# A two-layer transformer kernel: the first expert layer over tokens sorted by expert, with indirect DMAs

## The reference, cut to what matters

```python
n = layernorm(x)
x = x + attention_0(n) + experts_0(n)   # 8 heads, latent keys and values of 32, softmax over 1024
n = layernorm(x)
x = x + flow_attention_1(n) + experts_1(n)   # sums over tokens, no softmax; 8 experts, top 4, limits and biases

# experts_0: 8 experts, F = 256; each token t goes to two experts e with weights g from the router
y[t] = sum_e g[t, e] * (silu(n[t] @ w_gate[e].T) * (n[t] @ w_up[e].T)) @ w_down[e].T
```

## Time and profile before

| | |
|---|---|
| median of 3 runs | 3385.93 us (3384.25 to 3387.49) |
| the profiled execution | 3380.49 us |
| its span, first to last instruction | 3378.7 us |
| TensorE busy | 3081.9 us, 91% |
| VectorE busy | 2275.8 us, 67% |
| ScalarE busy | 1506.6 us, 45% |
| GpSimd (POOL) busy | 757.3 us, 22% |
| mean granted TensorE clock | 0.962 of 2.4 GHz |
| moved by DMA | 165.66 MB, 49 GB/s |

### The profile page before, as it was taken

One profiled execution on the slowest core, in us unless ns is written; L12 is line 12 of the kernel. 1 busy time (PEld: TensorE's weight loads), 2 busy tenths in 40 slices (PEclk: granted clock), 3 DMA queues, 4 the chain that ended last, 5 costly groups with the idle time before them and its releaser, 6 DMA issues.

```text
span 3378.7 us, 66006 instructions
## 1 busy us (share of the span) xinstructions
PE 3081.9 (91%) x21792; PEld 2160.6 (64%) x21792; DVE 2275.8 (67%) x3629; ACT 1506.6 (45%) x2490; POOL 757.3 (22%) x566
## 2 busy tenths in 40 slices
PE   4999789997899988999889988899889998999988
PEld 2776557765577655776567755677566775667755
DVE  3774677747776477764877648775497755977558
ACT  2663246722366224662246523565225642266422
POOL 0005230052300432004410134101350023500325
PEclk8999899998999999999999989999899998999989
DMA  5002110022100221002210012001120011200112
GB/s 213 8 27 76 60 48 8 27 75 70 44 3 30 72 82 33 27 10 67 85 30 27 21 56 91 24 27 32 45 94 21 27 45 63 69 15 27 57 57 69
DMA packets 81782, 165.66 MB, mean 49 GB/s; under 512 B 8271, under 2 KB 26904, under 8 KB 80920
## 3 DMA queue, kind: packets, MB, share of 16 engines
q1 hardware_dynamic: 81432, 161.11, 14.6%
HBM read 147.97 MB, written 13.11 MB: 48 GB/s over the span
## 4 chain that ended last, share of the span: by engine, by line
PE 72%; DVE 12%; issue 9%; ACT 3%; POOL 1%; DMA 1%; DVEq 1%; POOLq 0%; ACTq 0%; SPq 0%
PE ps L1146 17%; PE ps L1208 15%; PE ps L1227 12%; PE ps L1153 9%; PE ps L1241 8%; PE ps L1260 3%; DVE ffn_u L959 1%; PE ps L1173 1%; DVE probsT L977 1%; PE ps L1117 1%; DVE ffn_gu L1061 1%; DVE neg_max L857 1%; PE ps L1319 1%; ACT q_parts L565 1%; POOL probs L492 1%
## 5 line engine op out<-in xcount | busy, mean ns | idle before, releaser
L492 POOL TENSOR_TENSOR probs<-ffn_gu,gate_bc 128x512 f32<-128x512 f32 x416 | 555.1, 1336 | 2351.6 <-DVE ffn_gu L920 1843.0
L1146 PE MATMUL ps<-x_parts,w_split 128*128 128x512 f32 x3072 | 946.7, 444 | 82.8 <-DVE ffn_u L959 59.5
L1146 PEld LDWEIGHTS ps<-x_parts,w_split 128*128 128x128 f32 x3072 | 566.8, 189 | 399.9 <-issue 223.1
L857 DVE TENSOR_REDUCE neg_max<-ps 128x1 f32<-128x1024 f32 x512 | 626.0, 1223 | 237.0 <-PE ps L1208 141.1
L595 ACT ACTIVATE probs<-ps,neg_max 128x1024 f32<-128x1024 f32 x512 | 572.1, 1117 | 240.9 <-DVE neg_max L857 240.9
L1208 PE MATMUL ps<-keys,q_parts 128*128 128x512 f32 x2048 | 612.5, 421 | 21.1 <-DVE q_parts L850 11.4
L1227 PE MATMUL ps<-ident,probs 128*128 128x128 f32 x4096 | 543.1, 274 | 15.0 <-DVE probsT L868 13.9
L1227 PEld LDWEIGHTS ps<-ident,probs 128*128 128x128 f32 x4096 | 476.8, 141 | 104.2 <-DVE probsT L868 26.3
L1153 PE MATMUL ps<-probs,w_down 128*128 128x512 f32 x832 | 431.1, 604 | 46.0 <-POOL probs L492 45.2
L1208 PEld LDWEIGHTS ps<-keys,q_parts 128*128 128x128 f32 x2048 | 345.1, 188 | 168.9 <-issue 99.0
L920 DVE TENSOR_TENSOR ffn_gu<-ffn_s,ps 128x512 f32<-128x512 f32 x256 | 175.8, 687 | 330.7 <-ACT ffn_s L620 163.8
(11 more groups left out here) (171 smaller groups left out, 2517.5 us busy)
## 6 DMA issues: line engine op xcount, KB each, us to landing
w_split<-w_parts SPq DMA_DIRECT2D x260, 256.0 KB, 2.6
gate_bc<-gate_rows SPq DMA_DIRECT2D x128, 512.0 KB, 4.1
w_parts<-q_parts SPq DMA_DIRECT2D x4, 2048.0 KB, 9.3
x_in<-in_x SPq DMA_DIRECT2D x9, 512.0 KB, 3.7
out<-x_mid SPq DMA_DIRECT2D x8, 512.0 KB, 3.4
probsT<-in_gate_up SPq DMA_DIRECT2D x1, 2048.0 KB, 8.2
gate_bc<-in_gate_up SPq DMA_DIRECT2D x1, 2048.0 KB, 12.5
w_down<-in_down SPq DMA_DIRECT2D x2, 1024.0 KB
```

Of the source, the lines that this page charges most:

```text
L492: nc.gpsimd.tensor_tensor(ffn_h[u % 5], ffn_gu[:, u % 3, :], gate_bc[:, e % GATE_SLOTS, c * BANK:(c + 1) * BANK], ALU.mult).then_inc(h_rea ...
L857: nc.vector.tensor_reduce(neg_max[:, t % 4:t % 4 + 1], banks(2 * (t % 2)), X, ALU.max, negate=True).then_inc(max_ready.sem, 1)
L1146: mm = nc.tensor.matmul(ps[:, bank, :], w_split[:, f % 4, h, k * P:(k + 1) * P], tokens[:, half], start=(part == 0), stop=(part == 2))
```

## The change

- **Sorting.** The router now also marks the two experts chosen by each token. TensorE counts, with the matrices `before` and `ones`, how many earlier tokens chose the same expert. From that VectorE works out (`places`, two operations per step from step 40 on) a row number for each of the 2048 pairs of token and expert, such that every expert's rows begin at a multiple of 128, and for each of 23 blocks of 128 rows the number of its expert.
- **Scatter.** POOL writes the normed tokens to `x_rows` in HBM with 16 indirect DMAs of 128 rows. SP loads all 2944 rows back as `xs`.
- **Blocks** (`chosen_experts`). For each of 23 blocks TensorE reads the number of its expert from SBUF into a register (`value_load`) and makes three products with the tokens as the stationary and the weights as the moving operand, 512 columns (both halves of gate and up). The weights of layer 0 stay in SBUF (`w_res`). Silu and product are over 128x256, then two transposes, a copy, and two down products over 128 columns. Each group of four blocks has its tokens transposed and split ahead.
- **Back.** Each group's outputs are copied and stored to `y_rows`. When all six stores have landed, POOL reads them with 16 indirect DMAs, and VectorE multiplies by the token's two weights and adds.
- **Gone from layer 0**: the gates' transposes, their rows in HBM and the multiplication on POOL, the chunks of weights, and the transposes of the sums.
- **Attention.** `values` has two pieces of 32 matmuls in steps two apart. Where an instruction waits for two semaphores, the wait that is met earlier now stands first. VectorE's router operation stands behind the copy instead of ahead of it.
- **Memory.** `gate_bc`, `x_high` and `x_low` share memory with `q_parts`, and `xT` of layer 1 with `probsT`. The preparation splits the weights of layer 1 only by way of `w_prep`.

```diff
+BLOCKS = (2 * SEQ + E * (P - 1)) // P
+BLOCK_GROUPS = -(-BLOCKS // 4)
+TRANSPOSE_LAG = 2
+BLOCK_DOWN_LAG = 4
+GATHERS = 4
...
 SP, in the loop
+                sp.wait_ge(scattered.sem, scattered.at(b, 16 * 2 * NT))
+                sp.sem_inc(rows_complete.sem, 1)
+                sp.dma_start(xs, x_rows[:, :].rearrange("(j p) d -> p j d", p=P)).then_inc(xs_loaded.sem, 16)
+                for q in range(BLOCK_GROUPS):
+                    part = group_blocks(q)
+                    sp.wait_ge(ys_ready.sem, ys_ready.at(b, q + 1))
+                    sp.dma_start(y_rows[part[0] * P:(part[-1] + 1) * P, :].rearrange("(j p) d -> p j d", p=P),
+                                 ys[:, part[0]:part[-1] + 1, :]).then_inc(ys_stored.sem, 16)
...
 POOL, in the loop
+                pool.wait_ge(pos_ready.sem, pos_ready.at(b, 1))
+                nc.gpsimd.tensor_tensor(pool_spare[:, 0:1], minus_half[:, 0:1], minus_half[:, 0:1], ALU.mult)
+                for k in range(2):
+                    for n in range(NT):
+                        nc.gpsimd.indirect_dma_start(
+                            out=x_rows[:, :], out_offset=bass.IndirectOffsetOnAxis(pos_i[:, k * NT + n:k * NT + n + 1], 0),
+                            in_=x_norm[0][:, n, :], in_offset=None).then_inc(scattered.sem, 16)
+                inverse_deviation(b, 1)
+                pool.wait_ge(ys_stored.sem, ys_stored.at(b, 16 * BLOCK_GROUPS))
+                nc.gpsimd.tensor_tensor(pool_spare[:, 1:2], minus_half[:, 0:1], minus_half[:, 0:1], ALU.mult)
+                for n in range(NT):
+                    for k in range(2):
+                        nc.gpsimd.indirect_dma_start(
+                            out=y_pair[:, k, n, :], out_offset=None, in_=y_rows[:, :],
+                            in_offset=bass.IndirectOffsetOnAxis(pos_i[:, k * NT + n:k * NT + n + 1], 0)
+                        ).then_inc(gathered[n * GATHERS // NT].sem, 16)
+                inverse_deviation(b, 2)
...
 VectorE, behind the blocks
-                experts_add(0)
+                for i in range(GATHERS):
+                    tiles = range(i * NT // GATHERS, (i + 1) * NT // GATHERS)
+                    dve.wait_ge(gathered[i].sem, gathered[i].at(b, 16 * 2 * NT // GATHERS))
+                    for n in tiles:
+                        last = nc.vector.scalar_tensor_tensor(x_mid[:, n, :], y_pair[:, 0, n, :], r_s1[:, n:n + 1],
+                                                              x_mid[:, n, :], ALU.mult, ALU.add)
+                    link(last)
...
 TensorE, chosen_experts
+                def gate_up(j):
+                    if j % 4 == 0:
+                        pe.wait_ge(xs_low_ready.sem, xs_low_ready.at(b, j // 4 + 1))
+                    if j >= 2:
+                        pe.wait_ge(block_done.sem, block_done.at(b, j - 1))
+                    at = slice(j * P, (j + 1) * P)
+                    for part, (h, x) in enumerate(((0, 0), (0, 1), (1, 0))):
+                        mm = nc.tensor.matmul(ps[:, j % 2, :], xs_parts[x][:, at],
+                                              w_res_flat[:, bass.ds(first[j] * 4 + h * 2 * F, 2 * F)],
+                                              start=(part == 0), stop=(part == 2))
+                    mm.then_inc(block_mm.sem, 1)
...
+                for j in range(BLOCKS + BLOCK_DOWN_LAG):
+                    if j < BLOCKS:
+                        first[j] = pe.value_load(block_i[0:1, j:j + 1], min_val=0, max_val=(E - 1) * FH * D)
+                        gate_up(j)
+                    if j % 4 == 1 and j // 4 + 1 < BLOCK_GROUPS:
+                        tokens(j // 4 + 1)
+                    if 0 <= j - TRANSPOSE_LAG < BLOCKS:
+                        turn(j - TRANSPOSE_LAG)
+                    if j >= BLOCK_DOWN_LAG:
+                        down(j - BLOCK_DOWN_LAG)
+                    beside(j)
...
 TensorE, attention
-                    for k in (2 * i, 2 * i + 1):
+                    for k in range(4 * i, 4 * i + 4):
...
-                    for i in range(4):
-                        g = group_at(w, VALUES_LAG + i)
+                    for i in range(2):
+                        g = group_at(w, VALUES_LAG + 2 * i)
...
 VectorE, attention_step, one of the reordered pairs
-                        dve.wait_ge(scores_ready.sem, scores_ready.at(b, t + 1))
                         if t >= 4:
                             dve.wait_ge(exp_done.sem, exp_done.at(b, t - 3))
+                        dve.wait_ge(scores_ready.sem, scores_ready.at(b, t + 1))
```

More of the change, by code:

```diff
@@ L151, in two_layer_kernel @@
         x_mid = sb("x_mid", [P, NT, D])
-        xT = [sb(f"xT{l}", [P, SEQ]) for l in range(2)]
+        xT_first = sb("xT_first", [P, SEQ])
         stats = sb("stats", [P, NT, 6])
@@ new lines, in two_layer_kernel @@
+        gate_bc = q_flat[:, 0:GATE_SLOTS * SEQ].bitcast(F32).rearrange("p (s c) -> p s c", s=GATE_SLOTS)
+        gate_rows = nc.dram_tensor("gate_rows", (E, SEQ), F32, kind="Internal").ap()
+        ffn = sb("ffn", [P, 12, BANK])
+        ffn_flat = ffn[:, :, :].rearrange("p a b -> p (a b)")
+        w_raw = [v.rearrange("p (f c) -> p f c", c=2 * P) for v in (room[:, 4 * SEQ:8 * SEQ], ffn_flat[:, 0:4 * SEQ])]
+        ffn_s, ffn_g, ffn_gu = ffn[:, 0:3, :], ffn[:, 3:6, :], ffn[:, 6:9, :]
+        ffn_u = [ffn[:, 9, :], ffn[:, 10, :], out_room[:, :, :, :].rearrange("p a b c -> p (a b c)")]
@@ L234, in two_layer_kernel @@
+        xs_parts = [q_flat[:, h * 4 * SEQ:h * 4 * SEQ + ROWS] for h in range(2)]
+        ys = probs[:, :, :].rearrange("p a b -> p (a b)")[:, 0:ROWS].rearrange("p (j d) -> p j d", d=D)
+        y_pair = room[:, 5 * SEQ:7 * SEQ].rearrange("p (k n d) -> p k n d", k=2, d=D)
         ident = sb("ident", [P, P])
@@ L386, in _ @@
                          ).then_inc(x_loaded.sem, 16)
-            for l in range(2):
+            for l in (1, 0):
                 sp.dma_start(w_raw[l], ins[f"gate_up{l}"].rearrange("p f a b -> p f (a b)")).then_inc(raw_in[l].sem, 16)
@@ L442, in _ @@
+                for e in range(GATE_SLOTS):
+                    load_row(e)
+                for f in range(CHUNK_SLOTS, CHUNKS + CHUNK_SLOTS):
+                    if f % FH == 0 and GATE_SLOTS <= f // FH < E:
+                        load_row(f // FH)
+                    sp.wait_ge(gu_ready.sem, gu_ready.at(b, (f - CHUNK_SLOTS + 1) * HALVES))
+                    load_chunk(f)
                 sp.wait_ge(y_added.sem, y_added.at(b, 4))
@@ new lines, in outputs @@
+                def outputs(q):
+                    part = group_blocks(q)
+                    dve.wait_ge(ys_mm.sem, ys_mm.at(b, q + 1))
+                    nc.vector.tensor_copy(ys[:, part[0]:part[-1] + 1, :].rearrange("p j d -> p (j d)"),
+                                          ps[:, 5 + q % 2, 0:len(part) * D]).then_inc(ys_ready.sem, 1)
+                assert next(place, "end") == "end"
+                tokens_low(0)
+                for j in range(BLOCKS + BLOCK_DOWN_LAG + 1):
+                    if j < BLOCKS:
+                        if j >= 3:
+                            dve.wait_ge(hT_mm.sem, hT_mm.at(b, j - 2))
+                        dve.wait_ge(block_silu.sem, block_silu.at(b, j + 1))
+                        nc.vector.tensor_tensor(block_h[j % 3].rearrange("p (a c) -> p a c", a=FH),
+                                                block_s[j % 3].rearrange("p (a c) -> p a c", a=FH),
+                                                ps[:, j % 2, :].rearrange("p (a k c) -> p a k c", a=FH, k=2)[:, :, 1, :],
+                                                ALU.mult).then_inc(block_done.sem, 1)
+                    if j % 4 == 1 and j // 4 + 1 < BLOCK_GROUPS:
+                        tokens_low(j // 4 + 1)
+                    i = j - BLOCK_DOWN_LAG - 1
+                    if i >= 0 and (i % 4 == 3 or i == BLOCKS - 1):
+                        outputs(i // 4)
+                    attention_step(UNIT_STEP + j)
+                    if NORM_STATS <= j < NORM_STATS + NT // 2:
+                        k = j - NORM_STATS
```

556 lines of the change are left out of this document (337 added, 219 removed).

## The result

The changed kernel takes **3468.03 us** (median of 4 runs, 3457.48 to 3470.59), the kernel before on the same chip 3385.6: a ratio of 1.0237 (95% interval 1.0215 to 1.0259), so 2.4% slower. The prediction was 3353 and faster. The profiled span grew from 3378.7 to 3468.8 us, by 90.1.

The account below looks back on a forecast made before the run. TensorE was taken as the bound, time also being lost where chains leave it idle. Per image -5.9 - 20.6 + 23.9 = -2.6 us, -21 for eight, -12 once: -33, so about 3353 us; range 3240 to 3500.

Parts of the forecast that it names:

- Router and places: Routing and sorting beside attention: +1.1 us per image on TensorE, VectorE's operations just covered, POOL's scatters nothing.
- the four rivals: Alternative outcomes: slow gathers 3436 us (0.22), serial register load 3500 (0.12), both cheap 3253 (0.17), reordered attention bringing nothing 3409 (0.06).
- rivals 1 and 2: Way back: POOL gathers at 1.9 us, 3436 us, chance 0.22; blocks: register load in series, 3500 us, chance 0.12.
- Attention, -5.9 per image: Attention stage: values product -7.0 us plus the router's TensorE products +1.1 us per image.
- The values: Attention's values product: double pieces save 32 changeovers of 0.22 us, 7.0 us per image, nothing if VectorE can't follow.
- Waits reordered: Attention's reordered waits: a few hundredths of a us on VectorE and ScalarE beside TensorE's products, counted as nothing.
- Rival 4: Attention: the reordered attention brings nothing since VectorE sets the short steps, +56 us, 3409 us; chance 0.06.
- Experts, -20.6: First expert layer: 23 blocks of 2.1 us plus start and end, 55.5 us against 76.1 per image.
- The 0.3 for the register load: First expert layer: reading each block's expert number into TensorE's register adds 0.3 us to a block of 1.8.
- Rival 2: First expert layer: the register load stands in series, blocks of 2.9 us, +147 us, 3500 us; chance 0.12.
- Way back, +23.9: Last expert product to sums done: 28.1 us against 4.2 per image, 20 of it 16 POOL gathers at 1.25.
- Preparation, -11.7: Before image 1: first layer's weights converted without waiting for stores, TensorE's first part ending 31.3 instead of 42.95, once.

Follow-up runs that it names:

- no_scatter: The changed kernel with the 16 scatters and the two waits for them left out: 3311.44 us, ratio 0.9775.
- before_scatters: The kernel before with 16 back-to-back scatters of 128 rows added on POOL during attention, storing a constant tile nothing reads: 3520.51 us, ratio 1.0400.
- paced: The changed kernel with its 16 scatters issued one per attention step instead of back to back, full computation: 3307.03 us, ratio 0.9775.
- before_values: The kernel before with only the values of a group in two pieces of 32 matmuls instead of four of 16: 3369.96 us.
- spread_end: The paced kernel with each block's register load moved to the end of one of the last 23 attention steps: 3243.33 us, ratio 0.9594.

## Why the prediction was wrong

**The step that failed** is the one on POOL in "Router and places": "POOL's 16 scatters start near step 50 of 74, 60 us before they are needed ... Nothing." When they start and that they are done in time was right; that work on an idle engine costs the others nothing was not looked into. They cost 18.7 us per image (no_scatter), 17.1 alone (before_scatters): some 150 us, against a forecast of -33. None of the four rivals held it. That 3468 still lies in the range from 3240 to 3500 is luck: rivals 1 and 2, which drew its upper part, did not happen. Without this term the sign would have been right, and the gain over twice the forecast: -78 (paced) for -33.

**Attention, -5.9 per image.** The values were put at -7.0 on the ground that VectorE follows. It does so in the half of attention without the router, where they bring 0.66 us per group (0.44 predicted), and not beside the router as the kernel before had it: -1.0 in the stage (before_values). The prediction's own bound, "if VectorE can't follow, nothing", was the nearer. Its ground was a misreading: the "two operations of a step" that start 2.04 us apart in the earlier trace rows are the maxima of two steps, the second of which waited 0.22 us for TensorE, and the router's operation is not in that sum. (2.57 less 1.88 is 0.69, besides, not 0.66.) "Waits reordered: nothing" was wrong the other way, since they and the router's operation are what lets VectorE follow: 36.3 us of waiting fell back to 12.8, and both edits together brought -4.1. In paced, with the sorting's products, the stage came to -3.5. Nine groups in regular flow bring -5.5 there; the two in which the sorting's products stand take 1.6 longer, the queries between the halves 0.4 and the end 0.5, and the start 0.7 less. Rival 4 was near in size and wrong in its reason.

**Experts, -20.6.** -26.0 in image 2 (76.0 to 50.0). The 0.3 for the register load came out at 0.33, by luck: it was taken from the weight loader's idle at a changeover, where no register is loaded. The products of a block were mis-sized: 1.8 predicted, 1.37 to 1.5 measured, as two transposes and four down passes take 0.58 together (669.35 to 669.93 in spread_end), not 0.75, and nothing went to changeovers. Rival 2, with a load of 1.1 us in each block, did not happen: the load is 0.64 bare, and behind queued products half of it is hidden.

**Way back, +23.9.** Last down product to sums done 26.1 us (739.46 to 765.58) for 28.1, so +21.9. A gather took what was predicted, 1.25 (0.95 + 0.30), and 18.8 from the first start to the last; that too is luck, since 1.25 was the time of POOL's commonest elementwise operation, which has nothing in common with it. The 1 us of the Trainium skill (DMA: Bandwidth & Descriptors, Specifications) is a time to the first byte and not POOL's time for an issue, so the 16 us worked out from it were no price of the series, and a gather here landed 2.4 to 2.7 us after its issue. The rows were nearer. Most of the error is the landing of the last store, 2.6 us from the copy's start instead of 4.

**Preparation, -11.7.** -14.2 at the first query, once. With it the terms as measured without the hold-up, 8 x (-3.5 - 26.0 + 21.9) - 14, give -75, where paced has -78.

**The checks it named.** A group of four steps took 10.14 us (10.3 predicted, 10.74 before):
```profile
522.67 1.21 PE L1446 MATMUL ps<-keys,q_parts 128*128 128x512 f32 x4
524.51 1.18 PE L1446 MATMUL ps<-keys,q_parts 128*128 128x512 f32 x4
...
532.81 1.20 PE L1446 MATMUL ps<-keys,q_parts 128*128 128x512 f32 x4
```
That, the 16 entries of 1.25 us and the early first product came as forecast or better, and the total did not: the checks looked where the sum had terms.

## What to carry to other kernels

A transfer from an idle engine's queue isn't free because its engine is idle: look at what all other engines do while it is issued, and put at most two 128-row indirect DMAs back to back beside work, or one per step of the main loop. Here a register load cost TensorE 0.64 us where nothing was queued behind which to hide it, and nothing under a lump of 1 us of matmuls, so issue it steps ahead. When two edits touch the same loop, price them together: here the values needed the reorder to pay.

## What the runs showed of the hardware that was not expected

- A run of indirect DMAs on POOL (1.27 us each) holds up TensorE, VectorE and ScalarE from about the third on, in handoffs between engines (idle up to 7.2 us) and in matmuls with no wait among them (0.70 us apart). The first two are absorbed. It depends on the rows: 64 rows or 128 rows each do it, of 512 B and, at 128 rows, of 128 B too; 32 rows of 512 B don't; plain transfers of the same bytes at twice the rate don't.
- The Trainium skill (SBUF — State Buffer, SBUF: two separate sides) says that a DMA cannot be slowed by a compute instruction "and vice versa". That is a rule about ports, and no run here shows at which part of the chip the hold-up arises; but taken as a promise that transfers never slow compute it does not hold in this case: TensorE worked 10.8 of 22 us.
- POOL's time for an indirect DMA hardly depends on the rows: 0.88, 0.91 and 0.97 us for 32, 64 and 128.
- The clock follows: full until 609.4, eight us into the scatters, then at the lower of its two levels (1.2 of 2.4 GHz) until 629.9; granted 0.69 over the 22 us, in which TensorE worked 10.8, and 1.00 in the same stretch of paced.

What stays open is the mechanism. That single matmuls and semaphore handoffs are both late speaks for something that all engines share, instruction supply or the path of completions among them; the trace has one or two packets of instructions on each of two queues in such a stretch and doesn't tell them apart. Those packets take no longer than elsewhere (medians over all images 1.0 us against 1.1 on the one queue, 0.4 against 0.5 on the other), so if it is the supply of instructions, it isn't the time of its transfers.
